# VectorE's and ScalarE's order in a three-pass attention kernel: V's low parts before the sum tree, low parts of sums together, key bias in the second score product

## The chip, the cores and the metric

The kernel runs on one core of a Trainium2 chip. The metric is the device time of one execution in microseconds (us). The core has TensorE (PE, matrix products into the accumulator banks), VectorE (DVE), ScalarE (ACT), GpSimd (POOL) and SyncE (SP, which here only issues DMAs).

## What is computed

An attention block with group norm over 16 images of 512 channels and 32 x 32 pixels, all in float32:

```python
B, C, H, W = (16, 512, 32, 32);  GROUPS = 32;  EPS = 1e-05;  N = H * W
h = group_norm(x, gn_w, gn_b)
hf = h.reshape(B, C, N)
qkv = jnp.einsum('oc,bcn->bon', qkv_w, hf) + qkv_b[None, :, None]
q, k, v = jnp.split(qkv, 3, axis=1)
q = q.transpose(0, 2, 1)
v = v.transpose(0, 2, 1)
attn = jnp.einsum('bnc,bcm->bnm', q, k) * (1.0 / math.sqrt(C))
attn = jax.nn.softmax(attn, axis=-1)
o = jnp.einsum('bnm,bmc->bnc', attn, v).transpose(0, 2, 1)
o = jnp.einsum('oc,bcn->bon', out_w, o) + out_b[None, :, None]
return x + o.reshape(B, C, H, W)
```

## The kernel before

**Products in three passes.** Each float32 operand is split into a high part, rounded by a copy on ScalarE (`r_hi`, `h_hi`, ...), and a low part, the rest, by a subtraction on VectorE (`r_lo`, `h_lo`, ...). `three` (lines 260 to 264) issues three matmuls: high by high, high by low, low by high. So TensorE waits for low parts, and a low part for its high part.

**Preparation.** The weights are folded once: the query and key weights into one product, value and output weights into another (`u`). A batch is one image and takes 552 matmuls.

**Stages of a batch on TensorE** (lines 402 to 407), one behind the other, in eight accumulator banks (`ring`):

- T, 8 units of 12 matmuls (`t_units`): the folded key product by the normalised input `h`. Unit j may start when the output scaling j of the batch before has emptied its bank (`s_scaled`).
- scores, 7 products of 4 units of 6 matmuls (`score_products`): a 2 x 2 block product done with seven block products in place of eight (Strassen's way). Their stationary operands are the T blocks A11, A12, A22 ("direct": read from a bank) and the sums S1 to S4 of T blocks, their moving ones blocks of `h` or sums of these (the combined input, `h_combined`). The scores stand transposed, with keys on partitions, in 16 tiles of 128 x 512 in `stage`, eight for each half of the queries.
- V, 8 units of 12 matmuls (`v_units`).
- output half 0 and output half 1, 4 units of 24 matmuls each (`output_units`). In the first unit of half 0, step m waits for V's low part m (`s_vlo`) and for the pair m // 2 of the exponentials' low parts (`s_plo`).

**What the others do.** VectorE adds score products, keeps a running maximum, subtracts the maximum over all keys (GpSimd reduces it over the partitions, `max_all`), takes low parts of V (`v_rest`, line 875) and of the exponentials P (`p_rest`, 870), adds the exponentials up in a tree of three steps (`sum_tree`, 881 to 887), whose result GpSimd sums over the partitions (`sum_all`, 636). The sums go through DRAM to a reciprocal (`inverse`, 894), and the inverses through DRAM to all partitions (`inv`). `scale_output` (902) multiplies an output bank by them, and GpSimd issues the DMA that adds the result to the output in DRAM. The three buffers `scaled` go round, so scaling n waits until the DMA of scaling n - 3 has landed.

**The next image** is normalised meanwhile: statistics on VectorE (`stats_part`), their group's mean and variance (`group_variance`), the reciprocal root on GpSimd (`group_rstd`, line 656), its spread (`group_spread`, `affine_pair`); then ScalarE writes the full input and its high part (425, 421), VectorE its low part (`h_rest`, 724), the combined input (739 to 744), its low parts (748), and the product with the key direction (`key_dot`, 757 and 760), which GpSimd reduces over the partitions (623) and which becomes a bias of each key (`keybias`, 766).

**What sets the order.** Each engine runs the list of its block in the order in which it is written; semaphores tie the lists together. An engine that waits holds all behind it. `T_SUM` gives the step at which each sum is made; `s_tlo` counts the low parts of T blocks in the order of the lists, so a product's wait depends on that order:

```python
pe.wait_ge(s_tlo, b * 14 + 2 * a + 2)
```

## Time and profile before

| | |
|---|---|
| three runs | 2241.51, 2242.78, 2244.41 us; median 2242.78 |
| the profiled execution | 2240.99 us, its span 2239.2 us |
| TensorE | 2089.9 us busy (93%), 8956 matmuls, mean granted clock 0.961 |
| VectorE | 1619.2 us (72%) |
| ScalarE | 953.3 us (43%) |
| GpSimd | 415.6 us (19%) |

The span reaches from the first to the last instruction of the one profiled execution. Busy shares are means over stages. The granted clock is the share of TensorE's full 2.4 GHz: 1.00 is that, 0.50 is 1.2 GHz. Starts and durations in the rows are in us from the span's start.

### The profile page before, as it was taken

What the parts mean: (1) busy time and instruction counts of PE and PEld (TensorE: products, weight loads), DVE (VectorE), ACT (ScalarE), POOL (GpSimd) and SP (SyncE); (2) the same over time, 40 slices, a digit from 0 to 9 for tenths busy, and PEclk for the clock granted to TensorE, in tenths of its full rate; (3) what the DMA queues carried; (4) which work ended last, traced back from release to release, by engine and by line L of the source; (5) the groups of instructions that cost most, each with busy time, mean ns of one, the idle gap of its engine ahead of it and who ended that gap; (6) DMA issues with size and microseconds to landing.
All of it is one profiled execution on the core that took longest, in us unless ns stands there. A gap on an engine that the chain in (4) does not pass through costs nothing.

```text
span 2239.2 us, 23037 instructions
## 1 busy us (share of the span) xinstructions
PE 2089.9 (93%) x8956; PEld 1712.7 (76%) x8956; DVE 1619.2 (72%) x1949; ACT 953.3 (43%) x1179; POOL 415.6 (19%) x237
## 2 busy tenths in 40 slices
PE   8789999898998989989899898989989899898998
PEld 6668778686886868868687786878868688686886
DVE  7678677776767678676776867767777776767754
ACT  6353344434444343444433445334453444444341
POOL 2012030211302113030120302203021130211302
PEclk9899999999999999999999999999999999999999
DMA  5204122140321303213031220402214032130303
GB/s 156 77 5 78 42 43 81 16 108 1 48 77 27 98 1 48 77 29 95 1 56 68 38 86 6 96 23 44 81 20 104 1 48 76 29 95 1 48 38 48
DMA packets 88269, 118.37 MB, mean 53 GB/s; under 512 B 47824, under 2 KB 48432, under 8 KB 88160
## 3 DMA queue, kind: packets, MB, share of 16 engines
q0 software_dynamic: 19296, 35.92, 11.4%
q1 hardware_dynamic: 68864, 80.98, 11.0%
q8 instruction: 71, 1.16, 0.2%
q14 instruction: 38, 0.31, 0.0%
HBM read 46.78 MB, written 67.74 MB: 51 GB/s over the span
## 4 chain that ended last, share of the span: by engine, by line
PE 68%; DVE 16%; issue 6%; ACT 6%; POOL 2%; POOLq 0%; DVEq 0%
PE ring L262 23%; PE ring L263 23%; PE ring L264 23%; DVE stage L865 3%; ACT stage L510 3%; DVE r_lo L875 2%; DVE stage L846 2%; DVE run_max L858 2%; DVE r_lo L870 2%; DVE stage L881 2%; ACT r_hi L517 2%; POOL all_max L631 1%; ACT r_hi L522 1%; DVE stage L884 1%; DVE group_mv L908 1%
## 5 line engine op out<-in xcount | busy, mean ns | idle before, releaser
L262 PE MATMUL ring<-r_hi 128*128 128x512 f32 x1568 | 636.5, 406 | 128.7 <-DVE r_lo L875 120.0
L263 PE MATMUL ring<-r_lo,r_hi 128*128 128x512 f32 x1568 | 629.7, 402 | 0.0
L264 PE MATMUL ring<-r_hi,r_lo 128*128 128x512 f32 x1568 | 628.6, 401 | 0.0
L262 PEld LDWEIGHTS ring<-r_hi 128*128 128x128 f32 x1568 | 306.5, 195 | 210.7 <-DVE r_lo L875 137.5
L264 PEld LDWEIGHTS ring<-r_hi,r_lo 128*128 128x128 f32 x1568 | 306.1, 195 | 66.2
L263 PEld LDWEIGHTS ring<-r_lo,r_hi 128*128 128x128 f32 x1568 | 306.9, 196 | 63.0
L510 ACT ACTIVATE stage<-stage 128x1024 f32<-128x1024 f32 x128 | 135.5, 1058 | 450.3 <-DVE stage L865 448.5
L497 ACT ACTIVATE stage<-ring,keybias 128x512 f32<-128x512 f32 x256 | 173.0, 688 | 248.7 <-PE ring L264 248.7
L631 POOL PARTITION_ALL_REDUCE all_max<-run_max x32 | 57.2, 1787 | 943.8 <-DVE run_max L858 668.7
L846 DVE TENSOR_TENSOR stage<-stage,ring 128x512 f32<-128x512 f32 x192 | 131.5, 685 | 115.4 <-PE ring L264 62.6
L262 PE MATMUL ring<-h_hi,g_hi 128*128 128x512 f32 x512 | 199.4, 389 | 0.0
L264 PE MATMUL ring<-h_hi,g_lo 128*128 128x512 f32 x512 | 199.2, 389 | 0.0
L264 PE MATMUL ring<-u_hi,h_lo 128*128 128x512 f32 x512 | 199.2, 389 | 0.0
L263 PE MATMUL ring<-h_lo,g_hi 128*128 128x512 f32 x512 | 199.2, 389 | 0.0
L263 PE MATMUL ring<-u_lo,h_hi 128*128 128x512 f32 x512 | 199.2, 389 | 0.0
L262 PE MATMUL ring<-u_hi,h_hi 128*128 128x512 f32 x512 | 199.2, 389 | 0.0
L636 POOL PARTITION_ALL_REDUCE stage<-stage x32 | 129.8, 4056 | 340.6 <-DVE stage L887 180.7
L865 DVE TENSOR_TENSOR stage<-stage,all_max 128x1024 f32<-128x1024 f32 x128 | 183.3, 1451 | 0.0
L875 DVE TENSOR_TENSOR r_lo<-ring,r_hi 128x512 fp32r<-128x512 f32 x128 | 86.6, 687 | 116.8 <-ACT r_hi L522 116.8
L870 DVE TENSOR_TENSOR r_lo<-stage,r_hi 128x1024 fp32r<-128x1024 f32 x128 | 155.9, 1218 | 16.7 <-ACT r_hi L517 16.7
L858 DVE TENSOR_TENSOR run_max<-run_max,stage 128x512 f32<-128x512 f32 x192 | 137.8, 722 | 36.4 <-ACT stage L497 32.0
L262 PE MATMUL ring<-h_hi,r_hi 128*128 128x512 f32 x384 | 150.3, 391 | 14.7 <-DVE stage L833 14.7
(100 smaller groups left out, 3012.5 us busy)
## 6 DMA issues: line engine op xcount, KB each, us to landing
xs<-x_in SPq DMA_DIRECT2D x64, 512.0 KB, 6.0
out<-xs SPq DMA_DIRECT2D x64, 512.0 KB, 3.2
out<-run_max POOLq DMA_DIRECT2D x86, 256.0 KB, 4.3
out<-spare POOLq DMA_DIRECT2D x42, 256.0 KB, 4.5
inv<-inv_row SPq DMA_DIRECT2D x32, 256.0 KB, 3.8
stage<-stage POOLq DMA_DIRECT2D x3, 512.0 KB, 8.5
stage<-wk SPq DMA_DIRECT2D x4, 256.0 KB, 4.0
stage<-wq SPq DMA_DIRECT2D x4, 256.0 KB, 5.1
```

Of the source, the lines that this page charges most:

```text
L262: nc.tensor.matmul(ps_out, st_hi, m_hi, start=first, stop=False, skip_group_check=goes_on)
L263: nc.tensor.matmul(ps_out, st_hi, m_lo, start=False, stop=False, skip_group_check=goes_on)
L264: return nc.tensor.matmul(ps_out, st_lo, m_hi, start=False, stop=last, skip_group_check=goes_on)
L497: nc.scalar.activation(stage[:, to, :], ring[:, i, :], ACT.Identity, bias=keybias[:, m:m + 1]).then_inc(done, 1)
L510: nc.scalar.activation(here, here, ACT.Exp, scale=SCALE).then_inc(s_exp, 1)
L631: nc.gpsimd.partition_all_reduce(all_max[:, :], run_max[nb][:, :], P, bass.bass_isa.ReduceOp.max).then_inc(s_allmax, 1)
L636: nc.gpsimd.partition_all_reduce(stage[:, 8 * nb + 1, :], stage[:, 8 * nb, :], P, bass.bass_isa.ReduceOp.add).then_inc(s_allsum, 1)
L846: nc.vector.tensor_tensor(stage[:, to, :], stage[:, to, :], ring[:, CT + i, :], ALU.add).then_inc(done, 1)
L858: nc.vector.tensor_tensor(run_max[nb][:, :], first, stage[:, 8 * nb + m, :], ALU.max).then_inc(s_rmax[nb], 1)
L865: nc.vector.tensor_tensor(here, here, all_max[:, :].rearrange("p (o n) -> p o n", o=1).to_broadcast([P, 2, HALF]), ALU.subtract).then_inc( ...
L870: nc.vector.tensor_tensor(p_tiles(r_lo, nb, 2 * q, 2), stage[:, 8 * nb + 2 * q:8 * nb + 2 * q + 2, :], p_tiles(r_hi, nb, 2 * q, 2).bitcast ...
L875: nc.vector.tensor_tensor(v_part(r_lo, m), ring[:, m, :], v_part(r_hi, m).bitcast(FP32), ALU.subtract).then_inc(s_vlo, 1)
```

## The change

It moves instructions on VectorE and ScalarE and adapts what waits for them. Cut to its core:

```diff
+T_SPLIT = {A22: 0, A11: 2, A12: 4, S1: 6, S2: 8, S3: 10, S4: 12}
         def t_bank(b, j):
-            return (j + 1) % 8 if b == 0 else j
+            return (1, 2, 3, 4, 0, 5, 6, 7)[j] if b == 0 else j
...
-                            pe.wait_ge(s_tlo, b * 14 + 2 * a + 2)
+                            pe.wait_ge(s_tlo, b * 14 + T_SPLIT[a] + 2)
...
+            def copy_first(b, i):
+                act.wait_ge(s_bias_out, (b + 1) * DMA)
+                act.wait_ge(s_unit, b * UNITS + S0 + 4 * P_A11 + i + 1)
+                nc.scalar.activation(stage[:, i, :], ring[:, i, :], ACT.Identity).then_inc(s_p1, 1)
...
+            def add_first(b, i):
+                if i == 0:
+                    dve.wait_ge(s_kb, b + 1)
+                dve.wait_ge(s_p1, b * 4 + i + 1)
+                dve.wait_ge(s_unit, b * UNITS + S0 + 4 * P_A12 + i + 1)
+                nc.vector.scalar_tensor_tensor(stage[:, i, :], ring[:, CT + i, :], keybias[:, i:i + 1], stage[:, i, :],
+                                               ALU.add, ALU.add).then_inc(s_c11, 1)
```

ScalarE, in each batch: all direct high parts (A22, A11, A12) before those of the sums (S1 to S4), then `copy_first` without a wait for the key bias; in the first batch the direct ones of A22 and A11 also ahead of the copies of A21. In the second softmax half the copies of V tiles 6 and 7 (`v_hi_part`) move behind the second and the third exponential:

```diff
-                exponential(b, 1, 0)
-                p_part(b, 1, 0)
-                v_hi_part(b, 6)
-                v_hi_part(b, 7)
-                for q in range(1, CT):
+                for q in range(2):
                     exponential(b, 1, q)
                     p_part(b, 1, q)
+                v_hi_part(b, 6)
+                exponential(b, 1, 2)
+                p_part(b, 1, 2)
+                v_hi_part(b, 7)
+                exponential(b, 1, 3)
+                p_part(b, 1, 3)
```

VectorE: the low parts of all sums stand behind the direct ones, `key_bias` behind them, `add_first` in place of the first `add_scores`; `group_variance` moves ahead of the last four score adds; and from the middle of the softmax on:

```diff
                 v_rest(b, 4)
+                subtract_max(b, 1, 0)
+                subtract_max(b, 1, 1)
+                v_rest(b, 5)
+                subtract_max(b, 1, 2)
+                subtract_max(b, 1, 3)
+                v_rest(b, 6)
+                p_rest(b, 1, 0)
+                v_rest(b, 7)
                 if more:
                     group_spread(b + 1)
                 sum_tree(b, 0)
-                v_rest(b, 5)
-                subtract_max(b, 1, 0)
-                subtract_max(b, 1, 1)
-                v_rest(b, 6)
-                v_rest(b, 7)
+                p_rest(b, 1, 1)
+                p_rest(b, 1, 2)
+                p_rest(b, 1, 3)
                 if more:
                     affine_pair(b + 1)
-                p_rest(b, 1, 0)
-                subtract_max(b, 1, 2)
-                p_rest(b, 1, 1)
-                subtract_max(b, 1, 3)
-                p_rest(b, 1, 2)
-                p_rest(b, 1, 3)
                 sum_tree(b, 1)
```

Behind the second tree come three `h_rest`, `inverse(b, 0)`, the fourth `h_rest`, `h_combined`, the four scalings of half 0, `inverse(b, 1)`, the key dot, two low parts of the combined input, and then the scalings of half 1, the first of them followed by the third low part and the second by the fourth. (Before, scalings and `h_rest` alternated, and `inverse(b, 1)` and `h_combined` stood ahead of the fourth scaling.) At the start of the kernel the four low parts of the combined input stand ahead of the key dot, and in the first batch the low parts of A22 and A11 ahead of all sums.

VectorE in the softmax of a batch, from the low part of P's third pair of half 0 on. Rows with `r_lo<-ring` are V's low parts, those with `all_max` subtractions of the maximum, those with `group_pair` the root's spread, those at the end the tree. Before:

```order
L870 TENSOR_TENSOR r_lo<-stage,r_hi 128x1024
L875 TENSOR_TENSOR r_lo<-ring,r_hi 128x512
L870 TENSOR_TENSOR r_lo<-stage,r_hi 128x1024
L875 TENSOR_TENSOR r_lo<-ring,r_hi 128x512
L916 COPY group_pair<-group_mv 32x16
L917 COPY group_pair<-group_rstd 32x16
L881 TENSOR_TENSOR stage<-stage 128x2048
L884 TENSOR_TENSOR stage<-stage 128x1024
L887 TENSOR_TENSOR stage<-stage 128x512
L875 TENSOR_TENSOR r_lo<-ring,r_hi 128x512
L865 TENSOR_TENSOR stage<-stage,all_max 128x1024 x2
L875 TENSOR_TENSOR r_lo<-ring,r_hi 128x512 x2
```

The same place now, from the last low part of P's half 0 on:

```order
L886 TENSOR_TENSOR r_lo<-stage,r_hi 128x1024
L891 TENSOR_TENSOR r_lo<-ring,r_hi 128x512
L881 TENSOR_TENSOR stage<-stage,all_max 128x1024 x2
L891 TENSOR_TENSOR r_lo<-ring,r_hi 128x512
L881 TENSOR_TENSOR stage<-stage,all_max 128x1024 x2
L891 TENSOR_TENSOR r_lo<-ring,r_hi 128x512
L886 TENSOR_TENSOR r_lo<-stage,r_hi 128x1024
L891 TENSOR_TENSOR r_lo<-ring,r_hi 128x512
L932 COPY group_pair<-group_mv 32x16
L933 COPY group_pair<-group_rstd 32x16
L897 TENSOR_TENSOR stage<-stage 128x2048
L900 TENSOR_TENSOR stage<-stage 128x1024
```

V's tiles 5, 6 and 7 now stand ahead of the root's spread and of the tree, with four subtractions and one low part of P among them.

ScalarE in the same place, from the copies of V tiles 3 to 5 on (`r_hi<-ring`); `stage<-stage` is an exponential and `r_hi<-stage` its high part. Before:

```order
L522 ACTIVATE r_hi<-ring 128x512 x3
L510 ACTIVATE stage<-stage 128x1024
L517 ACTIVATE r_hi<-stage 128x1024
L522 ACTIVATE r_hi<-ring 128x512 x2
L510 ACTIVATE stage<-stage 128x1024
L517 ACTIVATE r_hi<-stage 128x1024
```

Now:

```order
L528 ACTIVATE r_hi<-ring 128x512 x3
L516 ACTIVATE stage<-stage 128x1024
L523 ACTIVATE r_hi<-stage 128x1024
L516 ACTIVATE stage<-stage 128x1024
L523 ACTIVATE r_hi<-stage 128x1024
L528 ACTIVATE r_hi<-ring 128x512
L516 ACTIVATE stage<-stage 128x1024
L523 ACTIVATE r_hi<-stage 128x1024
L528 ACTIVATE r_hi<-ring 128x512
```

Two exponentials with their copies now stand ahead of V tile 6, and three ahead of tile 7.

VectorE in the first batch, T blocks: `r_lo<-ring` is a direct low part, `stage<-ring` a sum, `r_lo<-stage` with 512 columns a sum's low part. Before:

```order
L748 TENSOR_TENSOR r_lo<-stage,r_hi 128x1024 x4
L816 SCALAR_TENSOR_TENSOR r_lo<-ring,t_bias,r_hi 128x512
L833 SCALAR_TENSOR_TENSOR stage<-ring,t_bias,stage 128x512
L816 SCALAR_TENSOR_TENSOR r_lo<-ring,t_bias,r_hi 128x512
L833 SCALAR_TENSOR_TENSOR stage<-ring,t_bias,stage 128x512
L839 TENSOR_TENSOR r_lo<-stage,r_hi 128x512 x2
L816 SCALAR_TENSOR_TENSOR r_lo<-ring,t_bias,r_hi 128x512
```

Now:

```order
L817 TENSOR_TENSOR out_bias<-ring,col 128x4
L823 SCALAR_TENSOR_TENSOR r_lo<-ring,t_bias,r_hi 128x512 x4
L840 SCALAR_TENSOR_TENSOR stage<-ring,t_bias,stage 128x512 x6
L823 SCALAR_TENSOR_TENSOR r_lo<-ring,t_bias,r_hi 128x512
L840 SCALAR_TENSOR_TENSOR stage<-ring,t_bias,stage 128x512
L823 SCALAR_TENSOR_TENSOR r_lo<-ring,t_bias,r_hi 128x512
L840 SCALAR_TENSOR_TENSOR stage<-ring,t_bias,stage 128x512
L846 TENSOR_TENSOR r_lo<-stage,r_hi 128x512 x8
```

The four low parts that the first product waits for are together and first, and the eight of the sums together and last.

## Rows read from the trace of the kernel before

**Rows 1.** TensorE's waits: engine, line, releaser: us in total, times, longest us.

```profile
PE ring L262 <- DVE r_lo L875: 120.0, 31, 5.3
```

**Rows 2.** Windows (length; busy us and count by engine; granted clock, DMA): output halves.

```profile
134.90:167.40 32.50, 24.96 (x97) 19.64 (x96) 23.30 (x24) 18.40 (x18) 8.93 (x3) 0.84 0.04 5
1089.70:1122.70 33.00, 25.49 (x98) 20.03 (x97) 23.30 (x24) 18.40 (x18) 8.90 (x3) 0.84 0.03 5
1122.70:1144.40 21.70, 21.70 (x97) 17.98 (x96) 20.40 (x18) 4.26 (x4) 8.72 (x5) 1.00 0.42 67
2181.60:2211.40 29.80, 24.63 (x98) 19.84 (x97) 21.44 (x22) 9.33 (x10) 7.02 (x3) 0.89 0.06 10
```

**Rows 3.** TensorE's time line: start, duration, what, [idle before, who ended it].

```profile
1097.91 0.80 PE L262 MATMUL ring<-r_hi 128*128 128x512 f32 x1 [4.63 <-DVE r_lo L875]
1102.43 0.80 PE L262 MATMUL ring<-r_hi 128*128 128x512 f32 x1 [2.87 <-DVE r_lo L875]
28.13 0.50 PE L262 MATMUL ring<-r_hi 128*128 128x512 f32 x1 [1.70 <-DVE r_lo L678]
```

**Rows 4.** Windows as in rows 2: the first batch's stall and products, a slow stretch.

```profile
58.60:73.40 14.80, 0.12 (x2) 0.04 (x1) 14.70 (x24) 6.62 (x12) 0.00 (x0) 0.65 0.04 1
73.40:113.20 39.80, 39.80 (x169) 32.82 (x170) 22.07 (x34) 15.70 (x21) 1.79 (x1) 0.96 0.30 108
1097.40:1107.50 10.10, 6.71 (x15) 4.83 (x16) 8.47 (x10) 5.09 (x6) 4.05 (x1) 0.50 0.01 2
```

**Rows 5.** VectorE's time line in the softmax of the eighth batch.

```profile
1088.39 0.68 DVE L875 TENSOR_TENSOR r_lo<-ring,r_hi 128x512 fp32r<-128x512 f32 x1
1092.84 0.17 DVE L916 COPY group_pair<-group_mv 32x16 f32<-32x16 f32 x1 [3.77 <-POOL group_rstd L656]
...
1096.57 0.69 DVE L887 TENSOR_TENSOR stage<-stage 128x512 f32<-128x512 f32 x1
1097.18 0.68 DVE L875 TENSOR_TENSOR r_lo<-ring,r_hi 128x512 fp32r<-128x512 f32 x1
1097.78 2.35 DVE L865 TENSOR_TENSOR stage<-stage,all_max 128x1024 f32<-128x1024 f32 x2
1101.69 1.29 DVE L875 TENSOR_TENSOR r_lo<-ring,r_hi 128x512 fp32r<-128x512 f32 x2 [1.56 <-ACT r_hi L522]
```

**Rows 6.** ScalarE's time line there.

```profile
1099.03 1.06 ACT L510 ACTIVATE stage<-stage 128x1024 f32<-128x1024 f32 x1 [11.73 <-DVE stage L865]
1100.12 1.06 ACT L517 ACTIVATE r_hi<-stage 128x1024 fp32r<-128x1024 f32 x1
1101.08 1.06 ACT L522 ACTIVATE r_hi<-ring 128x512 fp32r<-128x512 f32 x2
```

**Rows 7.** GpSimd's time line: the dot's reduction in the first batch, a first sum.

```profile
51.35 6.99 POOL L623 PARTITION_ALL_REDUCE stage<-stage  x1 [1.27 <-DVE stage L760]
...
1103.45 4.24 POOL L636 PARTITION_ALL_REDUCE stage<-stage  x1 [10.64 <-issue]
```

**Rows 8.** VectorE's time line: preparation, T blocks, and the tail of the eighth batch.

```profile
51.13 8.96 DVE L748 TENSOR_TENSOR r_lo<-stage,r_hi 128x1024 fp32r<-128x1024 f32 x4
...
64.69 1.40 DVE L833 SCALAR_TENSOR_TENSOR stage<-ring,t_bias,stage 128x512 f32<-128x512 f32 x2
...
1104.49 3.26 DVE L865 TENSOR_TENSOR stage<-stage,all_max 128x1024 f32<-128x1024 f32 x1
...
1117.70 0.17 DVE L894 RECIPROCAL own_inv<-own_sum 128x4 f32<-128x4 f32 x1
...
1123.86 0.69 DVE L902 TENSOR_TENSOR spare<-ring,inv 128x512 f32<-128x512 f32 x1 [4.87 <-DMA inv<-inv_row]
...
1135.17 3.92 DVE L760 SCALAR_TENSOR_TENSOR stage<-stage,k_dir 128x1024 f32<-128x1024 f32 x3
...
1139.61 6.44 DVE L748 TENSOR_TENSOR r_lo<-stage,r_hi 128x1024 fp32r<-128x1024 f32 x2
```

**Rows 9.** DMA issues of the page: count, KB each, us to landing.

```profile
out<-run_max POOLq DMA_DIRECT2D x86, 256.0 KB, 4.3
```

More of the change, by code:

```diff
@@ L313, in t_bank_free @@
                     pe.wait_ge(s_prod_lo[0], CT)
-                elif j < 6:
-                    pe.wait_ge(s_prod_lo[1], j - 2)
-                elif j == 6:
+                elif j < 7:
+                    pe.wait_ge(s_prod_lo[1], (1, CT, 2, 3)[j - 3])
+                else:
                     pe.wait_ge(s_vec_sb, 3)
-                else:
-                    pe.wait_ge(s_prod_lo[1], CT)
             def t_bank_read(b, bank):
@@ L524, in _ @@
             for b in range(B):
-                copy_a21(b, 0)
-                copy_a21(b, 1)
-                for kk in range(2):
-                    t_direct_part(b, A22, kk)
-                for kk in range(2):
-                    t_sum_part(b, S1, kk)
-                for kk in range(2):
-                    t_direct_part(b, A11, kk)
-                for a in (S2, S3):
+                if b > 0:
+                    for kk in range(2):
+                        copy_a21(b, kk)
+                for a in (A22, A11):
+                    for kk in range(2):
+                        t_direct_part(b, a, kk)
+                if b == 0:
+                    for kk in range(2):
+                        copy_a21(b, kk)
+                for kk in range(2):
+                    t_direct_part(b, A12, kk)
+                for a in (S1, S2, S3, S4):
                     for kk in range(2):
                         t_sum_part(b, a, kk)
-                for kk in range(2):
-                    t_direct_part(b, A12, kk)
-                for kk in range(2):
-                    t_sum_part(b, S4, kk)
-                act.wait_ge(s_kb, b + 1)
                 for i in range(CT):
-                    copy_scores(b, P_A11, i, i, i, s_p1)
+                    copy_first(b, i)
                 for k in range(CT):
@@ L764, in key_bias @@
             def key_bias(n):
+                if n == 0:
+                    dve.wait_ge(s_bqk, 1)
                 dve.wait_ge(s_bias_in, (n + 1) * DMA)
@@ L802, in _ @@
             h_combined(0)
+            for c in range(CT):
+                h_combined_rest(0, c)
             dve.wait_ge(s_vec_sb, 2)
@@ L807, in _ @@
             nc.vector.tensor_tensor(out_bias[:, :], ps_ob, col[:, BO:BO + CT], ALU.add).then_inc(s_vec_sb, 1)
-            for c in range(CT):
-                h_combined_rest(0, c)
-            dve.wait_ge(s_bqk, 1)
             def t_direct_rest(b, a, kk):
@@ L929, in _ @@
                 more = b + 1 < B
+                if b == 0:
+                    for a in (A22, A11):
+                        for kk in range(2):
+                            t_direct_rest(b, a, kk)
                 for kk in range(2):
-                    t_direct_rest(b, A22, kk)
+                    if b > 0:
+                        t_direct_rest(b, A22, kk)
                     t_sum(b, S1, kk)
@@ L936, in _ @@
                 for kk in range(2):
-                    t_sum_rest(b, S1, kk)
-                for kk in range(2):
-                    t_direct_rest(b, A11, kk)
+                    if b > 0:
+                        t_direct_rest(b, A11, kk)
                     t_sum(b, S2, kk)
                     t_sum(b, S3, kk)
-                for a in (S2, S3):
+                for kk in range(2):
+                    t_direct_rest(b, A12, kk)
+                    t_sum(b, S4, kk)
+                for a in (S1, S2, S3, S4):
                     for kk in range(2):
@@ L945, in _ @@
                 key_bias(b)
-                for kk in range(2):
-                    t_direct_rest(b, A12, kk)
-                    t_sum(b, S4, kk)
-                for kk in range(2):
-                    t_sum_rest(b, S4, kk)
                 for i in range(CT):
-                    add_scores(b, P_A12, i, i, s_p1, s_c11)
+                    add_first(b, i)
                     if i > 0:
@@ L964, in _ @@
                     max_step(b, 0, CT + i, CT + i, s_c21, b * 4 + i + 1)
+                if more:
+                    group_variance(b + 1)
                 for i in range(CT):
@@ L967, in _ @@
                     max_step(b, 1, CT + i, i, s_c12, b * 4 + i + 1)
-                if more:
-                    group_variance(b + 1)
                 subtract_max(b, 0, 0)
```

28 lines of the change are left out of this document (12 added, 16 removed).

## The prediction

> **What bounds the kernel now.** I read TensorE's list of waits first, then the busy time of single stages, then the time line of each engine around the stall. TensorE bounds the kernel: its one large wait is for the low parts of V, 120.0 us [rows 1]. In the batch that I follow (the eighth, from 1008 us; all times below are on its clock), the first output half takes 33.0 us where the second, of as many matmuls, takes 21.7 [rows 2]. The sixteen first halves are long by 32.5 - 21.7 = 10.8 us in the first batch, 8.1 in the last and 11.0 to 11.9 in between: 179.4 us in all ([rows 2] has the first, the eighth and the last of the 16). The time line shows two idle stretches, 4.63 and 2.87 us, each ended by a low part of V (tiles 5 and 6), and the clock at half speed, 0.50, from 1097.4 to 1107.5 [rows 3, 4]. The 15 matmuls of that stretch are busy for 6.71 us; at the pace of the second half (96 in 21.7 us) they would take 3.4, so it costs some 3.2 us. With 7.5 idle and two restarts (0.3 each) that makes the 11.3.
>
> Why VectorE is late: V tile 4 at 1088.39, then idle 3.77 us for GpSimd's group root, then the sum tree, and V tile 5 only at 1097.18; tiles 6 and 7 stand behind two subtractions and ScalarE's first exponential of that half, at 1101.69 [rows 5, 6]. The second stall is the first batch's: 14.8 us from 58.6 us, clock mean 0.65 [rows 4].
>
> **The change, part by part.** The instructions stay the same in number; only the score add gains a bias operand. The nearest row has that form, 1.40 us for two [rows 8]; 0.70 is about what the old form takes, and all 64 lie beside TensorE's work: nothing.
>
> *V's low parts.* I walk VectorE and ScalarE by the spacings of [rows 5, 6] (0.60 us for a 512-column tile, 1.13 for 1024; ScalarE 1.09 from exponential to its copy, 0.96 to the next, 0.47 after a V copy). The group variance (1.1 us) goes ahead of the last four score adds, where VectorE has slack to absorb part of it; I take 0.4 us of lead for all that follows. V tile 4 then starts at 1088.0, two subtractions at 1088.6 and 1089.7, V tile 5 at 1090.8. TensorE wants it at 1093.1: the first stall is gone, with the root's wait and the sum tree behind it. Late next is tile 6. ScalarE takes the first exponential at 1089.8 (the subtraction's start + 1.25 [rows 5, 6]), its copy at 1090.9, the second pair at 1091.85 and 1092.95, V tile 6 at 1093.9, the third pair at 1094.4 and 1095.5, V tile 7 at 1096.4. VectorE follows 0.61 later: tile 6 at 1094.5, tile 7 at 1097.0. TensorE starts 0.74 after VectorE does [rows 3, 5], so at 1095.25 and 1097.8. It is idle 1.5 us, works 0.8, is idle 1.7: with restarts 3.4 us lost where 11.2 were, **16 x 3.4 = 54 us instead of 179**.
>
> *The clock* in these two gaps: it did not fall in the 1.70 us of idleness at 26 us and fell in each of the long ones (4.6 us and more) [rows 3, 4]. Each new gap is no longer than the one that kept it, but only 0.8 us of work lies between them; no row shows such a pair. Bounds: 0, or the 3.2 us of half speed found above. I take 0, by the nearest row.
> The Trainium skill, "TensorE: Matmul & The Clock Gate", section "A second HAM failure mode: psum-queue depth-cycling", says that short idle times between groups of matmuls can by themselves make the clock go down and up; that would give the rival priced below, and no row here shows it.
>
> *Sums and root later.* The sum tree (4.26 us, to 1097.26 [rows 5]) now starts at 1097.8 and ends at 1102.05. GpSimd's first all-partition sum began 6.19 us after the tree's end (at 1103.45 [rows 7]; 6.0 to 6.4 in 15 batches), though it had been idle 10.64 since the root: I take it that the gap follows the tree. So it comes at 1108.3 to 1112.5, 4.9 us later than before. Behind it hang the sum's store, which frees the tiles for ScalarE's next full input (8 x 1.13 us from 1113.7), its low parts on VectorE (the fourth at 1124.1), the reciprocal at 1121.8, the inverses 6.1 us later (1117.70 to 1123.86 [rows 8]), the combined input at 1126.3 to 1131.1, three output scalings, and the fourth once the first's store has landed (0.7 for the scaling and 4.3 for the store [rows 9]) at 1136.1; then the key dot (some 4.7: 0.8 and the three steps of [rows 8]), and two low parts of the combined input. One of these starts just ahead of GpSimd's reduction of the dot and runs free, the next is held till it ends: the pair takes 6.44 us in one row, as a subtraction takes 3.26 instead of 1.2 under a reduction [rows 7, 8]. The scaling that frees the bank of the fifth T unit ends at 1147.9. TensorE, 7.8 us earlier in each batch than before, reaches that unit at 1089.7 + 2 x 21.7 + 3.4 + 10.9 = 1147.4. Idle 0.5 us and a restart: **15 x 0.6 = 9 us**. The walk is 50 us long and good to a microsecond or two; its price runs from 0 to 3 us a batch. If the clock does fall, TensorE comes 3 us later and this wait vanishes; the two don't add.
> The next scalings (1149.6, 1151.4) precede their units (1150.7, 1153.4).
>
> *T splits, sums later, key bias.* The first product now needs four low parts and not six, and the eight low parts of sums run together behind the direct ones. From TensorE's start of the products: the third product is wanted at +10.9, its parts are there by +7.5, and the first sum of scores, which frees its bank, ends at +8.2. The copies on ScalarE no longer wait for the bias but stand behind all splits, which moves the shift of the input, its four stores, four loads and the statistics by 1.5 us; they end at +22.8 and the next add is due at +24. Hidden, with 1.2 us left; beyond it the adds still have the banks' slack. No term.
>
> *First batch.* The key dot ends about 55.1 us, behind the four low parts, so GpSimd's 6.99 us reduction no longer holds these (8.96 us for four, 4.6 free [rows 7, 8]). Four direct low parts follow, then four sums, at 0.66 to 0.70 us each: the first product's bank is read at 60.5, and TensorE, done with T at 57.8, waits 2.8 us instead of 14.8 (the end of T moves by 0.1). The clock stays up, which saves another 1.6 (39.8 us of products at a mean of 0.96 [rows 4]): **13.6 us**. The reduction now lies beside these reads of banks. Bounds: not held (no row shows such a read begin under a reduction), or held like the 8.96 us row, 8 us less gain. I take the first, since its second operand only comes from the tile memory that the reduction reads.
> The Trainium skill, "SBUF — State Buffer", section "Who interferes with whom", says that a VectorE instruction with at most one SBUF input doesn't contend with GpSimd; by it the 13.6 stand, by a hold it would be 5.6.
>
> **The sum.** Span 2239.2 - (179.4 - 54.4) + 9 - 13.6 = 2109.6. The profiled run took 2240.99, 1.8 more than its span, and the median of the three is 1.8 above that: **2113 us**.
>
> **Rivals.**
> 1. *The clock falls in the pair of gaps.* For: only 0.8 us of work in 4 us, and once down it came back only 5 us after TensorE had resumed for good (1102.4 to 1107.5). Against: the gap at 26 us. Price 3.2 x 16 less the 9 us of the T wait: 2113 + 51 - 9 = 2155 if in all batches, 2125 to 2140 if in some.
> 2. *The tail is later than walked*, by 1 to 3 us a batch at the fifth T unit (both low parts held, or the store of the first scaling late): 2128 to 2158.
> 3. *It doesn't do what it says*: ScalarE's two pairs ahead of V tile 6 take the place of the tree. The walk has that at 1.5 us; if V tiles 6 and 7 waited for a second pair more each, 2 x 2 us plus the clock: 2113 + 16 x 7 - 9 = 2216. Against: the order of the copies is fixed.
> 4. *Slower than before.* One mechanism: the late first sum delays inverses and scalings until TensorE stands at the T units for longer than it gained. It gained 7.8 us a batch and has the first batch's 13.6: from (125 + 13.6) / 15 = 9.2 us at the fifth unit on it is slower. Two more 6.2 us gaps of the sum's kind (before the dot's reduction, too) would give 12: 2113 - 9 + 15 x 12.4 = 2290. Against: the dot's reduction began 0.2 us behind its dot in every batch; between them GpSimd only issues DMAs.
>
> **Chances.** Forecast 0.52, rival 1 0.28, rival 2 0.13, rival 3 0.02, rival 4 0.02, and 0.03 for better than forecast (the V chain tighter; no T wait gives 2104, half the V loss 2086). Forecast's own span is 2095 to 2125. The range, 2095 to 2155, holds that, rival 1 and most of rival 2. This kernel can be told from no change at about 0.2% (4.5 us): faster 0.965, same 0.01, slower 0.025.
>
> **What would show it.** Right: no wait for the root on VectorE; V tile 5 ahead of TensorE; two gaps of 1.5 and 1.7 us; first output half 25.1 us at a granted clock of 1.00 and a batch of some 129 us; GpSimd's first sum 6.2 us behind the tree; products starting near 60.6 us. Wrong: 0.50 in that stretch (rival 1), waits of TensorE for output scalings above 1 us (rival 2, 4), or a wait for score copies, which I have at none.

## The result

The changed kernel takes 2151.12 us (median of four runs, 2145.01 to 2152.79), the kernel before 2242.15 (four runs); the ratio is 0.959, 95% interval 0.9567 to 0.9612. It is faster by 91 us where 130 were forecast: 38 us above the forecast and inside the range of 2095 to 2155, but outside the 2095 to 2125 that the prediction gave to its forecast alone. The range held because it also covered the first two rivals, and each of these came true in part.

The page of the changed kernel, its span and TensorE's and VectorE's busy shares (VectorE is at 1614.5 us, hardly changed; TensorE waits less):

```profile
span 2150.2 us, 23262 instructions
...
PE 2063.4 (96%) x8956; PEld 1690.7 (79%) x8956; DVE 1614.5 (75%) x1949; ACT 937.9 (44%) x1179; POOL 424.0 (20%) x237
```

TensorE's list of waits after (line 263 is the first matmul of three, 891 a low part of V, 918 an output scaling), against [rows 1]:

```profile
PE ring L263 <- DVE r_lo L891: 46.1, 32, 1.6
PE ring L263 <- DVE run_max L918: 18.6, 10, 3.7
...
PE ring L263 <- DVE spare L918: 6.4, 5, 2.9
```

The wait for V's low parts fell from 120.0 to 46.1 us, two short ones in each of 16 batches. A wait that the kernel before didn't have takes its place in part: 25.0 us for output scalings, once in each of 15 batches.

Windows of the changed kernel as in [rows 2]: the first and the second output half of the eighth batch, its T stage, the first half of the ninth and of the last batch, and the T stage of the ninth. A T stage takes 21.8 us in the kernel before.

```profile
1043.60:1068.80 25.20, 22.28 (x97) 17.84 (x96) 20.71 (x22) 10.25 (x11) 7.51 (x3) 1.00 0.02 1
1068.80:1090.60 21.80, 21.80 (x98) 18.03 (x97) 11.51 (x12) 12.30 (x12) 3.66 (x4) 1.00 0.10 21
956.60:983.70 27.10, 23.35 (x97) 18.89 (x96) 24.50 (x26) 4.61 (x7) 11.26 (x6) 0.94 0.56 77
...
1178.30:1204.90 26.60, 23.69 (x98) 18.86 (x97) 20.77 (x23) 11.63 (x13) 8.54 (x3) 0.94 0.02 1
2098.00:2122.60 24.60, 22.34 (x98) 17.87 (x97) 19.80 (x17) 8.56 (x10) 7.10 (x2) 1.00 0.01 1
1090.60:1118.50 27.90, 24.99 (x98) 20.05 (x97) 24.63 (x26) 4.71 (x7) 11.29 (x7) 0.88 0.57 80
```

The stages can be added up from TensorE's matmuls over all 16 batches, each from its first matmul to the first of the next stage, in us:

| | before | after | difference | forecast |
|---|---|---|---|---|
| first output halves | 526.0 | 413.6 | -112.4 | -125 |
| T stage and stall of the first batch | 37.6 | 24.8 | -12.8 | -12 |
| T stages of the other 15 | 326.4 | 364.9 | +38.5 | +9 |
| scores | 611.0 | 609.4 | -1.6 | -1.6 |
| V, second output halves | 696.5 | 696.5 | 0 | 0 |
| ahead of the first T and behind the last matmul | 41.7 | 41.1 | -0.6 | 0 |
| span | 2239.2 | 2150.2 | -89.0 | -129.6 |

The trace lacks 40.6 us of the forecast gain. The T stages account for 29.5 of them and the first output halves for 12.6; the two lines for the first batch and the ends of the span give 1.4 back.

TensorE's time line at the two short V waits of the eighth batch, and at its fifth T unit:

```profile
1049.17 0.50 PE L263 MATMUL ring<-r_hi 128*128 128x512 f32 x1 [1.37 <-DVE r_lo L891]
...
1051.70 0.50 PE L263 MATMUL ring<-r_hi 128*128 128x512 f32 x1 [1.56 <-DVE r_lo L891]
...
1104.54 0.79 PE L263 MATMUL ring<-h_hi,g_hi 128*128 128x512 f32 x1 [2.91 <-DVE run_max L918]
```

The gaps in [rows 3] were 4.63 and 2.87. The last of these matmuls runs slow (0.79 against 0.50): the clock is down there, as the granted 0.88 of that T stage's window says.

### The profile page after: what moved, and what is told of

It is laid out like the page before. It is cut to its first block, busy times and chain, and to the rows that moved or that the text cites. A ratio compares the mean times of both kernels' runs of the same rounds, so it can differ in the third digit from the quotient of the medians.

```text
span 2150.2 us, 23262 instructions
## 1 busy us (share of the span) xinstructions
PE 2063.4 (96%) x8956; PEld 1690.7 (79%) x8956; DVE 1614.5 (75%) x1949; ACT 937.9 (44%) x1179; POOL 424.0 (20%) x237
## 4 chain that ended last, share of the span: by engine, by line
PE 40%; DVE 28%; ACT 15%; issue 7%; DMA 6%; POOL 2%; SPq 0%; DVEq 0%; ACTq 0%; POOLq 0%
PE ring L263 14%; PE ring L265 13%; PE ring L264 13%; ACT stage L516 5%; DVE r_lo L886 5%; DVE stage L881 3%; ACT r_hi L523 3%; DVE r_lo L891 3%; DVE stage L897 2%; DMA sum_row<-stage 2%; POOL stage L642 2%; DVE stage L862 2%; ACT stage L424 2%; DVE stage L766 2%; ACT h_hi L420 2%
## 5 line engine op out<-in xcount | busy, mean ns | idle before, releaser
L263 PE MATMUL ring<-r_hi 128*128 128x512 f32 x1568 | 619.5, 395 | 54.2 <-DVE r_lo L891 46.1
L264 PE MATMUL ring<-r_lo,r_hi 128*128 128x512 f32 x1568 | 615.0, 392 | 0.0
L265 PE MATMUL ring<-r_hi,r_lo 128*128 128x512 f32 x1568 | 615.0, 392 | 0.0
L263 PEld LDWEIGHTS ring<-r_hi 128*128 128x128 f32 x1568 | 297.6, 190 | 129.6 <-DVE r_lo L891 59.8
L265 PEld LDWEIGHTS ring<-r_hi,r_lo 128*128 128x128 f32 x1568 | 297.2, 190 | 62.5
L264 PEld LDWEIGHTS ring<-r_lo,r_hi 128*128 128x128 f32 x1568 | 297.6, 190 | 61.0
L503 ACT ACTIVATE stage<-ring,keybias 128x512 f32<-128x512 f32 x192 | 132.2, 688 | 227.6 <-PE ring L265 227.6
L263 PE MATMUL ring<-h_hi,g_hi 128*128 128x512 f32 x512 | 204.9, 400 | 25.0 <-DVE run_max L918 18.6
L424 ACT ACTIVATE stage<-xs,h_bias,h_scale 128x1024 f32<-128x1024 f32 x62 | 76.5, 1234 | 221.2 <-DMA sum_row<-stage 217.3
L642 POOL PARTITION_ALL_REDUCE stage<-stage x32 | 116.0, 3656 | 253.9 <-DVE stage L897 227.8
L486 ACT ACTIVATE r_hi<-ring,t_bias 128x512 fp32r<-128x512 f32 x96 | 66.1, 689 | 217.9 <-PE ring L265 217.9
L730 DVE TENSOR_TENSOR h_lo<-stage,h_hi 128x1024 fp32r<-128x1024 f32 x64 | 78.4, 1225 | 105.2 <-ACT h_hi L420 104.5
```

Source lines behind the costliest of these rows:

```text
L263: nc.tensor.matmul(ps_out, st_hi, m_hi, start=first, stop=False, skip_group_check=goes_on)
L264: nc.tensor.matmul(ps_out, st_hi, m_lo, start=False, stop=False, skip_group_check=goes_on)
L265: return nc.tensor.matmul(ps_out, st_lo, m_hi, start=False, stop=last, skip_group_check=goes_on)
L424: nc.scalar.activation(h_full[:, k, :], xs[:, k, :], ACT.Identity, bias=h_bias[:, k:k + 1], scale=h_scale[:, k:k + 1]).then_inc(done, 1)
L486: nc.scalar.activation(t_part(r_hi, a, kk), ring[:, t_bank(b, j), :], ACT.Identity, bias=t_bias[:, i:i + 1]).then_inc(s_thi, 1)
L503: nc.scalar.activation(stage[:, to, :], ring[:, i, :], ACT.Identity, bias=keybias[:, m:m + 1]).then_inc(done, 1)
```

## Where the walk held and where it slipped

VectorE's time line from V tile 5 on (1044.74), then tiles 6 and 7, the last step of the tree, and the tail: the reciprocal, the combined input, the fourth scaling, the two low parts of the combined input, the scaling for the fifth T unit. It answers to [rows 5, 8].

```profile
1044.74 0.68 DVE L891 TENSOR_TENSOR r_lo<-ring,r_hi 128x512 fp32r<-128x512 f32 x1
...
1048.43 0.69 DVE L891 TENSOR_TENSOR r_lo<-ring,r_hi 128x512 fp32r<-128x512 f32 x1 [0.74 <-ACT r_hi L528]
...
1050.95 0.69 DVE L891 TENSOR_TENSOR r_lo<-ring,r_hi 128x512 fp32r<-128x512 f32 x1 [0.70 <-ACT r_hi L528]
...
1055.28 0.69 DVE L903 TENSOR_TENSOR stage<-stage 128x512 f32<-128x512 f32 x1
...
1075.82 0.17 DVE L910 RECIPROCAL own_inv<-own_sum 128x4 f32<-128x4 f32 x1
...
1081.81 1.23 DVE L745 TENSOR_TENSOR stage<-stage 128x1024 f32<-128x1024 f32 x1 [3.64 <-DMA sum_row<-stage]
...
1091.89 0.69 DVE L918 TENSOR_TENSOR spare<-ring,inv 128x512 f32<-128x512 f32 x1 [3.52 <-DMA out<-spare]
...
1097.19 6.69 DVE L754 TENSOR_TENSOR r_lo<-stage,r_hi 128x1024 fp32r<-128x1024 f32 x2
1103.80 0.68 DVE L918 TENSOR_TENSOR run_max<-ring,inv 128x512 f32<-128x512 f32 x1
```

GpSimd's: the root, both sums (merged in one row), and the dot's reduction, against [rows 7].

```profile
1046.17 0.84 POOL L662 TENSOR_TENSOR group_rstd<-group_veps,minus_half 32x1 f32<-32x1 f32 x1 [7.51 <-issue]
1062.13 7.52 POOL L642 PARTITION_ALL_REDUCE stage<-stage  x2 [15.12 <-DVE stage L897]
...
1097.48 6.90 POOL L629 PARTITION_ALL_REDUCE stage<-stage  x1 [3.44 <-DVE stage L766]
```

Taken from the start of the first output half (1089.7 in the prediction's walk, 1043.6 here):

| | walk | trace |
|---|---|---|
| V tile 6, low part | 4.8 | 4.8 |
| V tile 7 | 7.3 | 7.35 |
| end of the first tree | 12.35 | 12.35 |
| first sum on GpSimd | 18.6 | 18.5 |
| reciprocal | 32.1 | 32.2 |
| combined input | 36.6 | 38.2 |
| fourth scaling | 46.4 | 48.3 |
| low parts of the combined input | 51.7 | 53.6 |
| scaling for the fifth T unit, start | 57.5 | 60.2 |

Up to the reciprocal the walk is right to 0.1 us. It slips at three places behind it, 2.7 us in sum. The combined input waits until the second sum's row has been stored; SyncE's time line has that store issued at 1079.11, 2.7 us before it lets the combined input go; the prediction names no such wait, and its combined input is 1.6 us earlier:

```profile
1078.75 0.32 SPq L236 DMA_DIRECT2D inv<-inv_row  x1
1079.11 0.29 SPq L225 DMA_DIRECT2D sum_row<-stage  x1
1081.81 0.32 SPq L227 DMA_DIRECT2D own_sum<-sum_row  x1
```

The first scaling's store let the fourth go 5.4 us after the first scaling's start and not 5.0, and the dot's reduction held the second low part for 0.8 us more than the walk had.

## The first batch

Windows of the scores and of T with its stall (against [rows 4], where the scores took 39.8 us at 0.96):

```profile
60.10:98.30 38.20, 38.20 (x169) 31.62 (x170) 29.76 (x48) 17.69 (x26) 2.64 (x2) 1.00 0.33 112
35.30:60.10 24.80, 22.91 (x106) 18.68 (x104) 23.04 (x29) 14.89 (x24) 8.90 (x5) 1.00 0.19 32
```

TensorE's time line at the matmul that ends the stall, then VectorE's with the four direct low parts and the sums behind them, then GpSimd's with the dot's reduction:

```profile
60.09 0.47 PE L263 MATMUL ring<-h_hi,r_hi 128*128 128x512 f32 x1 [1.89 <-DVE stage L840]
```

```profile
54.59 2.72 DVE L823 SCALAR_TENSOR_TENSOR r_lo<-ring,t_bias,r_hi 128x512 fp32r<-128x512 f32 x4
57.23 4.04 DVE L840 SCALAR_TENSOR_TENSOR stage<-ring,t_bias,stage 128x512 f32<-128x512 f32 x6
```

```profile
54.81 6.14 POOL L629 PARTITION_ALL_REDUCE stage<-stage  x1 [4.14 <-DVE stage L766]
```

Ten reads of accumulator banks follow each other every 0.66 us beside the reduction (54.81 to 60.95); nine of them begin under it. They were not held, as the prediction chose. The trace agrees here with the page "SBUF — State Buffer" of the Trainium skill, section "Who interferes with whom". The stall is 1.9 us, where 2.8 were expected.

## The experiments

All times are medians of four runs, with the ratio to the kernel before (2242 us in each comparison) and its 95% interval. "Fell" is the number of batches in which the clock was at half speed at some time in the stage. The stage columns are those of the one profiled execution of each kernel; the fastest of the changed kernel's four executions (2145.01 us) had a mean granted clock of 0.982, the profiled one 0.989, so another execution need not have its falls in the same batches or as many.

| kernel | us | ratio, interval | first halves, us (fell) | 15 T stages, us (fell) |
|---|---|---|---|---|
| before | 2242 | | 526.0 (16) | 326.4 (0) |
| changed | 2151.1 | 0.959, 0.9567 to 0.9612 | 413.6 (6) | 364.9 (5) |
| V's order alone | 2153.2 | 0.9606, 0.9591 to 0.962 | 441.1 (16) | 326.4 (0) |
| changed without V's order | 2218.0 | 0.9904, 0.9878 to 0.993 | 517.4 (16) | 326.4 (0) |
| T and first batch alone | 2227.9 | 0.9935, 0.992 to 0.995 | 527.0 (16) | 326.4 (0) |
| changed, old tail | 2125.6 | 0.948, 0.9466 to 0.9495 | 420.8 (8) | 326.4 (0) |
| the last with the variance late | 2143.1 | 0.956, 0.9544 to 0.9576 | 441.5 (16) | 326.4 (0) |
| changed, one scaling first | 2129.9 | 0.9503, 0.9489 to 0.9517 | 418.0 (7) | 334.8 (1) |
| changed, early load | 2123.0 | 0.9471, 0.9457 to 0.9485 | 420.9 (8) | 326.4 (0) |
| changed, V earlier | 2142.9 | 0.9551, 0.9535 to 0.9567 | 348.2 (0) | 426.0 (15) |
| V earlier, old tail | 2049.3 | 0.9141, 0.9128 to 0.9155 | 348.2 (0) | 326.4 (0) |
| V earlier, old tail, early load | 2049.8 | 0.9142, 0.9129 to 0.9156 | 348.2 (0) | 326.4 (0) |

### V's order alone

The kernel before with only this of the change, on VectorE and ScalarE:

```diff
                 v_rest(b, 4)
-                if more:
-                    group_spread(b + 1)
-                sum_tree(b, 0)
-                v_rest(b, 5)
                 subtract_max(b, 1, 0)
                 subtract_max(b, 1, 1)
+                v_rest(b, 5)
+                subtract_max(b, 1, 2)
+                subtract_max(b, 1, 3)
                 v_rest(b, 6)
+                p_rest(b, 1, 0)
                 v_rest(b, 7)
+                if more:
+                    group_spread(b + 1)
+                sum_tree(b, 0)
...
                 v_hi_part(b, 5)
-                exponential(b, 1, 0)
-                p_part(b, 1, 0)
+                for q in range(2):
+                    exponential(b, 1, q)
+                    p_part(b, 1, q)
                 v_hi_part(b, 6)
+                exponential(b, 1, 2)
+                p_part(b, 1, 2)
                 v_hi_part(b, 7)
...
```

Expected: 

> The kernel before with one part of the change: the order of V's low parts on VectorE and of V tiles 6 and 7 on ScalarE; the tail (input, combined input, scalings) in the old order, T sums and first batch as before. Theory (V's order carries the gain, the new tail order causes the T waits of the changed kernel): the first output half falls from 33.0 to about 25.6 us (the group variance is late, so the pair of gaps is 0.4 longer in sum), no wait at the fifth T unit since the reciprocal no longer stands behind three low parts of the input; the first batch's 14.8 us stall stays: about 2135 us. Rival (the late first sum, not the tail order, makes the T waits): T stages of 23 to 28 us as in the changed kernel, about 2170 us.

Measured 2153.2 us. No T wait, so the rival is out: with the sum tree as late as in the changed kernel, the old tail keeps every T stage at 21.8 us. But the first halves take 27.0 to 28.6 us (26.1 in the last batch), not 25.6, since the clock fell in all 16 batches. TensorE's time line of this kernel at the first batch's pair of gaps:

```profile
141.34 0.50 PE L262 MATMUL ring<-r_hi 128*128 128x512 f32 x1 [1.74 <-DVE r_lo L877]
...
143.86 0.79 PE L262 MATMUL ring<-r_hi 128*128 128x512 f32 x1 [1.55 <-DVE r_lo L877]
```

The first gap is 0.37 us longer than the changed kernel's, the second the same, and the matmul behind it begins at half speed.

### The changed kernel without V's order

The same edit backwards, in the changed kernel. Expected: 

> The changed kernel with V's low parts and ScalarE's V tiles 6 and 7 put back in the old order. Theory: the first output half is back at about 33 us and the T waits are gone, since the sum tree is early again and TensorE late; what is left of the gain is the first batch: about 2228 us. Rival (other parts of the change carry some of the gain): clearly under 2220 us.

Measured 2218.0 us (2215.7 to 2227.6): the first halves are back at 29.6 to 33.2 us and the T waits are gone. It is 10 us under the theory. Against "T and first batch alone", which differs from it by the early variance and the tail, the first halves are shorter by 9.6 us in sum; in three middle batches the clock was low for a shorter time (6.8 and not 10.2 us). So something small helps here too, as the rival had it, but V's order carries the gain. The early variance is the likely cause; no run tells it from the tail here.

One half of the theory fails. VectorE's time line of this kernel at the scaling for the fifth T unit of the ninth batch:

```profile
1132.11 0.68 DVE L916 TENSOR_TENSOR run_max<-ring,inv 128x512 f32<-128x512 f32 x1
```

It starts 60.2 us behind the start of the output half (1071.9), as late as in the changed kernel, though the first sum on GpSimd is 5.3 us earlier here (13.2 us behind that start against 18.5). ScalarE's later exponentials now hold the full input up instead. The T wait is gone only because TensorE is late: it reaches the fifth T unit 63.8 to 65.9 us behind the start of the half, in the changed kernel 58.1 to 60.7; the scaling ends at 60.5 to 61.8 here and at 59.4 to 61.8 there.

### T and the first batch alone

The kernel before with `T_SPLIT`, the T and first-batch order on both engines, `copy_first` and `add_first`. Expected: 

> The kernel before with one part of the change: the T splits, the sums' low parts together, the key bias in the second product, the first batch's order; V's order, the variance and the tail as before. Theory: the first products start near 60 us and not at 73.4, the clock doesn't fall there, nothing else moves: 14 to 15 us less than before, about 2228 us. Rival (the key bias or the later input shift costs or gains in every batch): a batch period other than 136.5 us.

Measured 2227.9 us, 14.3 less than before. From the second batch on the batches take 136.2 to 136.8 us (133.3 the last), against 136.0 to 136.9 (133.3) before: the joined key bias, the splits and the later shift of the input cost and gain nothing in a batch. One thing differs from the theory: the clock did fall after the first batch's stall. TensorE's time line and a window behind it, of this kernel, and then the same window of the changed kernel:

```profile
59.67 0.47 PE L263 MATMUL ring<-h_hi,r_hi 128*128 128x512 f32 x1 [1.84 <-DVE stage L838]
```

```profile
59.70:63.00 3.30, 3.30 (x10) 2.60 (x11) 3.30 (x6) 2.71 (x5) 0.83 (x1) 0.63 0.06 6
```

```profile
59.70:63.00 3.30, 2.91 (x13) 2.44 (x14) 3.30 (x6) 2.85 (x6) 1.25 (x1) 1.00 0.02 6
```

One gap of 1.84 us brought the clock down here; one of 1.89 us at the same place of the changed kernel did not. Ten of the kernels here have this gap, at 1.80 to 1.91 us, and the clock fell behind it in six.

### The old tail

The changed kernel with this undone, from the second tree on:

```diff
-                if more:
-                    for k in range(CT - 1):
-                        h_rest(b + 1, k)
                 inverse(b, 0)
                 if more:
-                    h_rest(b + 1, 3)
-                    h_combined(b + 1)
-                for c in range(CT):
-                    scale_output(b, 0, c)
+                    h_rest(b + 1, 0)
+                scale_output(b, 0, 0)
+                if more:
+                    h_rest(b + 1, 1)
+                scale_output(b, 0, 1)
...
                         key_dot(b + 1, k)
-                    h_combined_rest(b + 1, 0)
-                    h_combined_rest(b + 1, 1)
                 scale_output(b, 1, 0)
+                if more:
+                    h_combined_rest(b + 1, 0)
+                    h_combined_rest(b + 1, 1)
...
```

Expected: 

> The changed kernel with the old order of the tail only: the reciprocal right behind the second tree, scalings between the input's low parts. Theory (the tail order makes the T waits): the reciprocal comes some 6 us earlier, the scaling for the fifth T unit some 10 us earlier, every T stage takes 21.8 us: 2151 - 38 = 2113 us. Rival (the late first sum makes them): T stages stay at 23 to 28 us and the time at 2150 us.

Measured 2125.6 us: 25.5 faster than the changed kernel. In the profiled executions, which are 28.0 us apart, the T stages lose all of their 38.5 us (364.9 to 326.4); 7.2 come back in the first halves, where the clock now falls in 8 batches and not 6, and 3.3 ahead of and in the first batch's scores, where it fell at two short gaps (1.93 and 1.86 us). VectorE's time line at the scaling for the fifth T unit of the ninth batch:

```profile
1078.32 0.68 DVE L918 TENSOR_TENSOR run_max<-ring,inv 128x512 f32<-128x512 f32 x1
```

It ends 46.7 us behind the start of the output half (1032.3), 14.2 earlier than in the changed kernel and 11 before TensorE comes for the bank; the theory had some 10 us earlier. TensorE's wait in this kernel that recurs in the batches is V's:

```profile
PE ring L263 <- DVE r_lo L891: 46.0, 32, 1.6
```

So, with V's new order, the new tail order costs 25 us of the gain. The late sum tree alone, with the old tail, costs nothing.

### The late variance

The kernel with the old tail, and `group_variance` back behind the last score adds. Expected: 

> a4_old_tail with the group variance back behind the last score adds, where it stood before: the only step between a1_v_only and a4_old_tail that touches the softmax. Theory (the early variance gives 0.4 us of lead, and with it also the clock): the first gap of the V pair is 1.9 us instead of 1.5 and the clock falls in every batch instead of in half of them; first output halves average 27.5 us instead of 26.3, about 2145 us. Rival (the lead is worth its 0.4 us and no more): 2126 + 6 = 2132 us.

Measured 2143.1 us, 17.4 more. The first halves take 441.5 us against 420.8 in sum, and the clock falls in 16 batches instead of 8. The first gap of a pair is 0.45 us longer, start to start, than with the early variance, which makes 7 of these 20.7 us in 16 batches; the other 14 go with the clock's falls. With "V's order alone", which also has the late variance, it agrees (441.1).

### One scaling ahead

```diff
                         key_dot(b + 1, k)
+                scale_output(b, 1, 0)
+                if more:
                     h_combined_rest(b + 1, 0)
                     h_combined_rest(b + 1, 1)
-                scale_output(b, 1, 0)
-                if more:
                     h_combined_rest(b + 1, 2)
                 scale_output(b, 1, 1)
```

(in the changed kernel). Expected: 

> The changed kernel with one move in the tail: the first scaling of output half 1 ahead of the two low parts of the combined input, of which the second is held under GpSimd's reduction. Theory (these two, 6.6 us, are the piece of the tail that makes the T waits): the scaling follows the key dot at once, 6 us earlier, T stages 21.8 us and the time as with the whole old tail, 2120 to 2127 us. Rival (the late reciprocal and the store in front of the fourth scaling matter as much): a wait stays or moves to the next scalings, 2135 to 2145 us.

Measured 2129.9 us. TensorE's waits for scalings in this kernel:

```profile
PE ring L263 <- DVE run_max L918: 2.4, 2, 1.3
PE ring L263 <- DVE spare L918: 2.3, 1, 2.3
```

4.7 us in three listed waits, where the changed kernel has 25.0 us in fifteen. The two low parts ahead of the scaling, one of them held under the reduction, were the decisive piece; the time lies between the two expectations, and a rest of the T stages' loss stays (8.4 us of 38.5). The three listed waits stand at the sixth T unit: its scaling now comes behind three low parts of the combined input in a row.

### The early load

```diff
                                             ALU.pow).then_inc(s_grstd, 1)
+                    nc.gpsimd.partition_all_reduce(idle_sum[:, :], bb_sum[:, :], P, bass.bass_isa.ReduceOp.add)
```

(in the changed kernel, behind the group root on GpSimd). Expected: 

> The changed kernel with one more instruction on GpSimd: a reduction of a 128 x 1 tile over the partitions right behind the group root, whose result nobody reads. Theory (the 6.2 us between tree and first sum is spent when GpSimd turns from the root to a reduction, and only once the reduction's operands are there): the small reduction takes that time while GpSimd is idle, the first sum begins 0.2 us behind its tree and 6 us earlier, the scaling for the fifth T unit 5 to 6 us earlier, T stages 21.8 us: about 2115 to 2120 us. Rival (the gap belongs to the sum itself): first sum still 6.2 us behind the tree, 2150 us.

Measured 2123.0 us. GpSimd's time line of this kernel: the root, the small reduction, the first sum.

```profile
1033.91 1.58 POOL L663 TENSOR_TENSOR group_rstd<-group_veps,minus_half 32x1 f32<-32x1 f32 x1 [6.77 <-issue]
1041.64 1.10 POOL L665 PARTITION_ALL_REDUCE idle_sum<-bb_sum  x1 [6.15 <-issue]
1044.66 4.04 POOL L643 PARTITION_ALL_REDUCE stage<-stage  x1 [1.93 <-DVE stage L905]
```

The small reduction waited 6.15 us for nothing but its own start, and the first sum, which had begun 6.2 us behind its tree, began 0.2 us behind the tree's last step (1043.76, 0.69 us long). The first sum is 5.9 us earlier against the start of its output half, the scaling for the fifth T unit behind the eighth batch ends 4.8 us earlier (56.1 against 60.9), and all T waits are gone, with the new tail order in place. So the T wait needs three things: the new tail order, the 6.2 us that GpSimd spends in front of its first sum, and a TensorE that V's new order has made early. Taking away any one of them removes it.

### V earlier

The changed kernel with V further ahead (VectorE, then ScalarE):

```diff
                 v_rest(b, 4)
-                subtract_max(b, 1, 0)
-                subtract_max(b, 1, 1)
                 v_rest(b, 5)
+                v_rest(b, 6)
+                subtract_max(b, 1, 0)
+                subtract_max(b, 1, 1)
+                v_rest(b, 7)
                 subtract_max(b, 1, 2)
                 subtract_max(b, 1, 3)
-                v_rest(b, 6)
                 p_rest(b, 1, 0)
-                v_rest(b, 7)
...
                 v_hi_part(b, 5)
-                for q in range(2):
-                    exponential(b, 1, q)
-                    p_part(b, 1, q)
                 v_hi_part(b, 6)
-                exponential(b, 1, 2)
-                p_part(b, 1, 2)
+                exponential(b, 1, 0)
                 v_hi_part(b, 7)
-                exponential(b, 1, 3)
-                p_part(b, 1, 3)
+                p_part(b, 1, 0)
+                for q in range(1, CT):
+                    exponential(b, 1, q)
+                    p_part(b, 1, q)
```

Expected: 

> The changed kernel, with V moved further: ScalarE copies V tiles 3 to 6 in a row and tile 7 behind the first exponential of the half, VectorE takes the low parts of tiles 4, 5, 6 ahead of any subtraction of that half and of tile 7 behind two of them. Theory: the low parts are there before TensorE wants them, so the first output half is 21.8 us in every batch at full clock (66 us less than the changed kernel in all), but TensorE then reaches the fifth T unit 3.5 us earlier and its scaling only about 1.5 us: the T wait grows from 1.6 to some 3.7 us a batch plus the clock's falls, about 2125 to 2150 us. Rival (the T waits come from something that moves with TensorE): T stages as in the changed kernel and about 2085 us.

Measured 2142.9 us: 8 less than the changed kernel, although every first output half now takes 21.8 us, 65 us less in sum. TensorE's waits for scalings in this kernel:

```profile
PE ring L263 <- DVE run_max L916: 40.7, 10, 4.9
PE ring L263 <- DVE spare L916: 22.1, 5, 4.9
```

62.8 us in 15 batches, 4.2 each, and the clock falls in every one of them: the T stages grow by 61 us. Nearly the whole gain went into the next wait.

### V earlier with the old tail

Both edits. Expected: 

> The changed kernel with V moved further as in b2_v_earlier and the tail in the old order as in a4_old_tail. Theory (with V's pair of gaps and the T waits gone nothing else waits in a batch): batches of 125.1 us, TensorE at full clock throughout, 2126 - 70 = about 2055 us. Rival (TensorE, now 3.5 us earlier, meets the next limit on VectorE, the T scalings or the score adds): batches of 127 to 129 us, 2085 to 2115 us.

Measured 2049.3 us, 4.7% less than the changed kernel. Page of this kernel:

```profile
span 2046.7 us, 23262 instructions
...
PE 2030.8 (99%) x8956; PEld 1679.9 (82%) x8956; DVE 1608.0 (79%) x1949; ACT 939.5 (46%) x1179; POOL 398.9 (19%) x237
```

Batches 2 to 15 take 125.1 us each and the last 125.3, none with a wait. With the early load on top (

> As b7_v_early_old_tail, with the small reduction of b4_early_load. Theory: equal to it within 0.2%, since the tail no longer bounds anything, about 2055 us. Rival (the sum's time still bounds the T scalings there): faster than it by 1 to 3 us a batch.

) it takes 2049.8 us: the same, as the theory had it, since the tail no longer bounds anything.

## Why the prediction was right, and where not

- **The V stall** (179 to 54 us): right in mechanism and, without the clock, in size. The idle times were forecast at 1.5 and 1.7 and are 1.37 and 1.56 in the rows, the undisturbed first half is 25.2 against a forecast 25.1. The order alone gives 89 us.
- **The clock in the pair of gaps**: taken at 0, and rival 1 at 3.2 us for each batch. It fell in 6 of 16 batches and cost 1.3 to 2.6 us in each (26.6 against 25.2 in the windows), some 10 us in all. Neither bound was the case; the choice by the one gap at 26 us was the failing step. At that very place of the kernel with the old tail a gap of 1.93 us brought the clock down, while in "V's order alone" one of 2.10 us did not, so the rows of one kernel can't tell how often such gaps do it. The Trainium skill, "TensorE: Matmul & The Clock Gate", section "A second HAM failure mode: psum-queue depth-cycling", has short idle times between groups of matmuls make the clock go down and up. The runs agree with it in part of the batches.
- **The T wait**: found, and at the right unit, and mis-sized: 9 us forecast, 38.5 measured. 25.0 are idle (1.7 a batch against 0.5); the rest are the restarts and the clock, which fell in 5 of the 15 T stages. The 0.5 was the small difference of two sums of nearly 60 us, and with the tail's slips, 2.7 us behind the eighth batch, the wait is 2.9 there and 1.7 in the mean. That was rival 2 (1 to 3 us a batch, 2128 to 2158), and 2151 lies in it: it should have had more than 0.13, as every slip of such a chain goes the same way once the wait is there.
- "If the clock does fall, TensorE comes 3 us later and this wait vanishes; the two don't add": right in direction, not in size. Where the clock fell in the V pair (6 batches), TensorE came to the fifth T unit 1.3 to 2.6 us later and the next wait was 0.78 us in the mean, with no fall in that T stage. Where it did not (9 batches with a T stage behind them), the wait was 2.25 us, and all 5 falls in T stages lie there, behind waits of 2.07 us and more. First half and next T stage together take 49.8 us with a fall in the pair and 50.6 without. So in this kernel a fall in the pair costs nothing net; what was wrong is that the wait vanishes, as the slips had made it longer than a fall is.
- **GpSimd's gap follows the tree**: right (18.5 us from the half's start against 18.6), and the early load shows that it belongs to the engine's turn from root to reduction and not to the sum.
- **The first batch**: 12.8 + 1.6 against 12 + 1.6. Shown by the kernel with that part alone (14.3).
- **Splits, sums, key bias in the other batches**: no term, and none found.
- **The lead of 0.4 us** from the early variance: right as a time (the walk's V tiles came to 0.1 us), but undoing it costs 17 us, most of it through the clock, which the prediction didn't see.
- What the forecast missed as a lever: with the old tail the same V order is 25 us better. The prediction named the chain, laid its delay to the late sum, and never asked what the old tail would do with the late sum.

## What to carry to other kernels

Where moving work ahead of a stall frees the bounding engine, walk the chain that has become later to its end and compare it with the new, earlier time of the bounding engine. A difference under 2 us at the end of such a walk is no slack: this one slipped by 2.7, and its cost grew by the clock's falls. Put the instruction that frees a resource for TensorE ahead of any that GpSimd can hold. A turn of GpSimd from one kind of work to another can be paid while it is idle, by a small instruction of the next kind.

## What the runs showed that I had not expected

- The granted clock can fall to 0.50 after a single gap of 1.84 us (0.63 in the window behind it) and stay up after one of 1.89 at the same place of another kernel; behind gaps of 1.80 to 1.91 us there, it fell in six kernels of ten. Pairs of 1.37 and 1.56 us with 1.0 us of work between them (1049.17 to 1050.14 in the eighth batch) brought it down in 6 of 16 batches (8 of 16 with the old tail), pairs of 1.74 and 1.55 (V's order alone) in 16 of 16, and so did the nearly equal ones of the kernel with the late variance. The length of a gap alone doesn't decide.
- GpSimd's 6.2 us ahead of a reduction that follows another kind of work begin only when the reduction's own wait is over: idle for 15.12 us in front of the first sum, it still began 6.2 us behind the tree. Where the small reduction had nothing to wait for, they passed at once (6.15 us).
- A VectorE instruction with both inputs in the tile memory that begins under GpSimd's reduction ends at about its end: the second of the pair of 6.69 us takes 5.56 us and ends 0.5 us before the reduction's recorded end. Ten instructions with one input in an accumulator bank ran beside a reduction at their own pace.
